# An attention and expert layer on one core: the idle TensorE products behind the loop are left out

## What is computed

```python
scores = jax.nn.sigmoid(x @ router_w.T)
G = jnp.einsum('ecd,edi->eci', Xp, W_gate)
U = jnp.einsum('ecd,edi->eci', Xp, W_up)
Y = jnp.einsum('eci,eid->ecd', jax.nn.silu(G) * U, W_down)
```

## The kernel before

| constant | products | place |
|---|---|---|
| WARM_HEADS | 3 | line 1316, ahead of the scores of head 2 |
| WARM_TILE | 2 | line 1339, ahead of the transposes of tile 1 |
| WARM_LAST | 3, twice | line 1341, behind the transposes of each tile |
| WARM_CHOICE | 3 | line 1368, behind `shared_hidden(0)` |
| WARM_ROWS | 4 | line 1376, behind the three products of the places |

## Time and profile before

### The profile page before, as it was taken

The page is one execution under the profiler, slowest core; times in us unless marked ns, Lnnn a source line. Parts: engine busy times, 40 slices in busy tenths (PEclk is TensorE's granted clock), DMA queues, the critical chain, the costliest instruction groups (busy, mean ns, idle before and its releaser), DMA issues.

```text
span 650.2 us, 15227 instructions
## 1 busy us (share of the span) xinstructions
PE 625.8 (96%) x6032; PEld 462.3 (71%) x6032; DVE 388.8 (60%) x554; ACT 363.6 (56%) x524; POOL 179.0 (28%) x146
## 2 busy tenths in 40 slices
PE   8999999999999999999999999999999999999976
PEld 5866666777777777777778777899556797564433
DVE  5979587766766766767767767556125885401001
ACT  4542765767677676676677667787123884311000
POOL 0260335354353353453443433300001231000000
PEclk9999999999999999999999999999999999999979
DMA  9943894224323323423422422500999006499995
GB/s 349 417 173 80 216 318 100 56 57 83 71 54 74 77 52 70 83 50 65 90 48 60 98 49 54 107 1 9 413 415 378 32 6 251 149 396 412 417 418 218
DMA packets 28072, 105.14 MB, mean 162 GB/s; under 512 B 4224, under 2 KB 8064, under 8 KB 22784
## 3 DMA queue, kind: packets, MB, share of 16 engines
q1 hardware_dynamic: 28032, 104.57, 50.3%
HBM read 77.29 MB, written 0.52 MB: 120 GB/s over the span
## 4 chain that ended last, share of the span: by engine, by line
PE 74%; DVE 8%; issue 5%; SPq 4%; ACT 4%; DMA 4%; POOL 1%; DVEq 0%; ACTq 0%
PE psO L1124 9%; PE psO L1135 9%; PE psO L1125 8%; PE psS L1111 8%; PE psS L1112 8%; PE psM L1083 5%; PE psO L1203 4%; PE psO L1067 3%; PE psS L1412 3%; DVE arena L779 2%; SPq L448 2%; PE psO L1069 2%; PE psO L1068 2%; DMA arena<-rope 2%; DMA arena<-w_exp 2%
## 5 line engine op out<-in xcount | busy, mean ns | idle before, releaser
L779 DVE TENSOR_REDUCE arena<-psM 128x2 f32<-128x1024 f32 x121 | 147.7, 1221 | 66.3 <-PE psM L1083 66.0
L588 ACT ACTIVATE arena<-psS 128x1024 bf16<-128x1024 f32 x128 | 131.4, 1026 | 87.5 <-PE psS L1112 85.4
L481 POOL TENSOR_TENSOR arena<-arena 128x1024 bf16<-128x1024 f32 x56 | 120.8, 2156 | 190.3 <-ACT arena L590 166.8
L1124 PE MATMUL psO<-arena 128*128 128x129 bf16 x1024 | 132.8, 220 | 0.3 <-DVE arena L797 0.3
L1125 PE MATMUL psO<-arena 128*128 128x128 bf16 x1024 | 132.4, 220 | 0.0
L590 ACT ACTIVATE arena<-psS 128x1024 f32<-128x1024 f32 x129 | 130.9, 1015 | 0.0
L1111 PE MATMUL psS<-arena 128*128 128x256 bf16 x512 | 120.5, 273 | 0.9 <-DVE arena L790 0.9
L1112 PE MATMUL psS<-arena 65*128 65x256 bf16 x512 | 120.8, 273 | 0.0
L1124 PEld LDWEIGHTS psO<-arena 128*128 128x128 bf16 x1024 | 99.1, 98 | 18.8 <-issue 11.2
L1125 PEld LDWEIGHTS psO<-arena 128*128 128x128 bf16 x1024 | 99.4, 97 | 6.8
L818 DVE TENSOR_TENSOR arena<-arena 128x1024 bf16<-128x1024 f32 (+1 forms) x73 | 88.0, 1207 | 15.4 <-ACT arena L590 15.3
(11 more groups left out here) (206 smaller groups left out, 747.3 us busy)
## 6 DMA issues: line engine op xcount, KB each, us to landing
arena<-w_exp SPq DMA_DIRECT2D x27, 1024.0 KB, 19.5
arena<-arena SPq DMA_DIRECT2D x96, 256.0 KB, 3.7
arena<-w_exp SPq DMA_DIRECT2D x31, 512.0 KB, 16.6
arena<-w_pair SPq DMA_DIRECT2D x8, 1088.0 KB, 19.1
arena<-w_exp SPq DMA_DIRECT2D x22, 256.0 KB, 6.4
arena<-w_o SPq DMA_DIRECT2D x1, 4096.0 KB, 21.6
arena<-ctx SPq DMA_DIRECT2D x4, 512.0 KB, 13.0
arena<-rope SPq DMA_DIRECT2D x4, 512.0 KB, 14.3
```

What stands on the lines that cost most here:

```text
L481: nc.gpsimd.tensor_tensor(p_lo[:, s % 2, :], p_f[:, s % 2, :], p_hi[:, s % 2, :], ALU.subtract).then_inc(s_plo[0], 1)
L588: nc.scalar.activation(p_hi[:, s % 2, :], psS[s % 2][:, :], ACT.Exp).then_inc(s_phi, 1)
L779: nc.vector.reduce_max(maxes[:, :, st, c], maxima_bank(q, m)[:, :].rearrange("p (j n) -> p j n", j=2), AX.X).then_inc(s_mfree, 1)
L1124: mm(psC[:, st, :], ph, vx[:, GROUP * g + i, 0:CW], start=g == 0 and i == 0 and st == 0, stop=False, skip_group_check=True)
```

## The change

The eighteen idle products behind the loop are left out: 3 + 2 + 2 x 3 + 3 + 4. The fourteen at the start stay. No other instruction, wait or transfer is changed.

```diff
--- before.py
+++ after.py
@@ -108,7 +108,7 @@
 DVE_BEFORE = order("rows0 q0 rows1 rope0 rows2 q1 k0 rows3 q2 rope1 m0 k1 rope2 rope3 k2 m1 m2 q3 k3 m3 m4 m5 q4 k4 m6 m7 m8 q5 "
                    "k5 m9 m10 k6 m11 m12 q6 m13 k7 m14 m15 q7")
 PAIR_BUFS = 6
-WARM_START, WARM_HEADS, WARM_TILE, WARM_LAST, WARM_CHOICE, WARM_ROWS = 14, 3, 2, 3, 3, 4
+WARM_START = 14
 
 
 def expert(k):
@@ -1312,8 +1312,6 @@
                     queries(h)
                 if 1 <= h <= TT:
                     values(h - 1)
-                if h == 3:
-                    warm(WARM_HEADS, psM[:, 0:512])
                 if 0 <= h - 1 < NH2:
                     scores2(h - 1)
                 if 0 <= h - 3 < NH2:
@@ -1335,10 +1333,7 @@
 
             pe.wait_ge(ld_route, 32)
             for st in range(TT):
-                if st:
-                    warm(WARM_TILE, psF[1])
                 xn_transposed(3, st)
-                warm(WARM_LAST, psF[1])
                 pe.wait_ge(ln_T, 2 * TT + st + 1)
                 for c in range(DC):
                     last = mm(psA[0][:, E * st:E * st + E], xnT[:, c, P * st:P * st + P], w_router[:, c, :], start=c == 0, stop=c == DC - 1)
@@ -1365,7 +1360,6 @@
                         mm(psO[n][:, D // 2 * st:D // 2 * (st + 1)], hs[:, i, P * st:P * st + P], sd[:, i, halves[n]],
                            start=i == 0 and st == 0, stop=False, skip_group_check=True)
             shared_hidden(0)
-            warm(WARM_CHOICE, psF[1])
             pe.wait_ge(sel_done, 1)
             pe.wait_ge(ld_const, 32)
             early, ones = const[:, C_EARLY:C_EARLY + P], const[:, C_ONES:C_ONES + P]
@@ -1373,7 +1367,6 @@
             mm(psA[1][:, 0:E], early, chosen[:, 0, :], start=True, stop=True)
             mm(psA[1][:, E:2 * E], ones, chosen[:, 0, :], start=True, stop=False)
             mm(psA[1][:, E:2 * E], early, chosen[:, 1, :], start=False, stop=True).then_inc(pos_mm, 1)
-            warm(WARM_ROWS, psF[1])
             pe.wait_ge(cleared, 2)
 
             def chosen_rows(part, c):
```

## The result

The changed kernel takes 654.69 us (653.22 to 655.73), beside 652.32 for the kernel before in the same series: ratio 1.0031, interval 1.0022 to 1.0040. It is slower by 2.4 us, inside the stated range of 651.2 to 654.9. They are not the quotients of the two medians, and differ from them by up to 0.1%.) The forecast had the wrong sign: no change, 0.2 us down. The profiled execution took 655.16 us.

The account below looks back on a forecast made before the run. The last 80 us were taken as one weight transfer, started when the first gate_up products free ring space. Six terms, five of 0 and one of 0.15 us, gave 651.9 against the profiled 652.05, 652.5 against the median; range 651.2 to 654.9.

Parts of the forecast that it names:

- the first release: First gate_up products free a quarter of four ring buffers at 563.5; only what moves this moves the end.
- HEADS: Three products at 505.66, ahead of head 2's score (L1267), which waits for GpSimd's L527: saved 0.
- CHOICE: Three products at 558.64, ahead of L1373, which waits for VectorE's choice of experts (L910): saved 0.
- TILE: Two products at 552.09, ahead of tile 1's transposes, which VectorE's L733 releases: saved 0, at most 0.05 us.
- both LAST: Three products at 550.33 and three at 553.36, ahead of the router's L1344, which waits for ScalarE's L546: saved 0.
- ROWS: Four products at 560.49 hold up L1385, which could start once the first one-hot (L952) is there: saved 0.15 us.
- D: All eighteen products lie open, the waits not being what the trace's releasers say: 3.9 us faster, 648.2; chance 0.06.
- I take it that the clock holds: Router stage, 549.9 to 555.1: the clock stays at 2.4 GHz though TensorE's busy share drops to 0.64; chance 0.56.
- B: Clock falls in the router stage, 553.4 to 555.4, for 6.8 us: +2.2 us, 654.25; +0.55 if half as long; chance 0.28.
- No DMA is moved: Whole kernel: no DMA moved and no wait added; expert 12's half and the stores stay, so no cost was counted.
- holes behind 566: Sign: holes in the DMA engines' full stretch behind 566 would refute the claim that only one release counts.
- E: Clock falls behind the gaps at 558.81 and 560.65; first gate_up takes twice its 0.99 us: +0.85, 652.9; chance 0.05.

Follow-up runs that it names:

- run 4: Changed kernel with half of shared_hidden(0) (its up part, 4 of 8 products) left out, output incomplete; 655.32 us against 652.39, ratio 1.0038.
- run 3: Kernel before with its eighteen idle products behind the loop kept in place, but 8 columns wide instead of 512; 654.48 us against 652.39, ratio 1.0034.
- run 1: Kernel before with only WARM_TILE and WARM_LAST kept of the eighteen; HEADS, CHOICE and ROWS left out; 653.11 us against 652.39, ratio 1.0016.
- run 2: Kernel before with only the eight idle products of the two router tiles (WARM_TILE, WARM_LAST) left out; 654.47 us against 652.39, ratio 1.0033.
- run 7: Changed kernel with the half of expert 12 issued by ScalarE's queue instead of the sync queue; 654.00 us against 652.57, ratio 1.0032.
- run 15: Kernel before, idle products included, with 220 satisfied waits more on TensorE in the first 60 us; 655.15 us, ratio 1.0038.
- control with 60: Kernel before with 60 satisfied waits more on TensorE in the first 60 us; 652.89 us, ratio 1.0006.
- run 13: Changed kernel with 60 satisfied waits more on TensorE in the first 60 us; 654.72 us against 652.35, ratio 1.0026.
- run 8: Kernel before with only the three idle products of WARM_CHOICE left out; 652.48 us against 652.57, ratio 1.0005.
- run 11: Kernel before with only the four idle products of WARM_ROWS left out; 652.82 us against 652.23, ratio 1.0006.
- run 5: Kernel before with one wait more in the sync queue, so the half of expert 12 is issued later; 653.64 us against 652.57, ratio 1.0010.
- run 10: The changed kernel measured again, unaltered; 654.14 us against 652.23, ratio 1.0027.
- run 16: The changed kernel measured a third time, unaltered; 654.67 us against 652.35, ratio 1.0028.
- run 9: Changed kernel with satisfied waits ahead of each tile's transposes, 18 instructions added instead of the 36 meant; 654.01 us against 652.23, ratio 1.0028.

## Why the prediction was wrong

**What bounds the kernel, and the way to the end: right.** Everything ahead of the first release comes through to the end (doubled `shared_hidden(0)`: 2.85 in, 2.87 out). That nothing can be saved in the tail was right too: the changed kernel's tail still waits for its weights.

**The six terms: right but for one size.** HEADS, CHOICE: 0, by their own runs (0.9998 and 1.0005). TILE and both LAST: 0; in the changed kernel L1007 and both L1339 start behind the releasers named, L733 and L546. ROWS: 0.06 and not 0.15. L1385 starts 0.45 us behind L952, when the first one-hot has been there for 0.15; what holds it for these 0.15 no run parts. D, all eighteen open, falls with them.

**The step that failed: "I take it that the clock holds".** It rested on comparing 5.2 us at a busy share of 0.64 with two stretches of other shapes at full clock, 0.74 and 0.54, and on no gap being over 1.0 us, when the only fall in the trace came in a standstill. Neither comparison carries over. The second of those rows is no safe case either: in the kernel without WARM_ROWS the clock fell at 643.5, at the end of such a stretch, of the same products (2.12 of 4.00 us busy from 639.6 on), though with longer gaps, up to 1.45 us. Instead of a clock that holds, the runs showed a fall to 1.2 GHz in eight of nine profiles without the eight products at full width: 6.8 us in three, 3.4 in four, 13.7 in that of run 4. The narrow products show that the work in the gaps decides, and runs 1 and 2 that the eight products of the router stage are the ones. For the two long falls B had the place (554.4; measured 554.0 to 554.5), the length (6.8 us) and the end of the dense group (562.2; 556.07 + 6.13 = 562.20). It gave +2.2 us; the two long falls cost 2.02 and 1.89. For a low level half as long it gave +0.55; the execution with 3.4 us shows 0.46, but otherwise than B had it: there L1339 is at full clock, L1351 ends 1.69 us late, and 0.99 of these are covered by the wait for L910. The chances, 0.56 for a clock that holds and 0.28 for B, were the wrong way round; no row of the trace had a stretch of this make at full clock.

The rule that the prediction cited against itself, in the Trainium skill, "TensorE: Matmul & The Clock Gate", section "A second HAM failure mode: psum-queue depth-cycling", holds here for the fall: the trace agrees, with a fall behind gaps of 0.5 to 0.7 us. A swing that repeats itself the runs do not show in this stage.

**The term that was missing: about 1 us.** "No DMA is moved" was true of the kernel's own transfers alone. The program's instructions come by DMA too, and one fetch moved from an idle moment onto the second issue. Two things move it there, each by itself: another count of instructions at full clock (run 7, and the 220 of run 15), and a low clock at the same count (run 3). The changed kernel has both. The prediction had named the sign ("holes behind 566"), and with it its claim that only the first release counts falls: the second issue stands on the same path. That a fetch moved onto the issues makes the second one long is shown by the kernel with 220 instructions, against its control with 60, and by all eighteen profiles (below). The cost is about 1 us by the means above, 0.96 against 0.31 in that pair of profiles. Why the issue waits for the fetch is open. So is where a fetch falls: with the clock low it came later than the count of instructions says (runs 3 and 13).

**E** was real, but does not show in the changed kernel: there the clock has just risen, from 561 on, when the gaps of the choice come (whether that is the reason was not tested). It shows when the router stage is repaired (run 1: first `gate_up` 1.85 us and not 1.06, medians +0.7 us). WARM_CHOICE and WARM_ROWS cover each other; either can go, not both, by runs 1, 8 and 11 (one profile each).

**The size.** The sum of B's +2.0 and the fetch's +1.0 would be 3.0, as in the profile of the result; the medians say 2.4, 1.9 and 2.3 in three series. The three profiles of the changed kernel show +3.06, +1.31 and +2.54: the low level lasts 3.4 us in one and 6.8 in two. No version tried beats the kernel before.

## What to carry to other kernels

An idle product that fills a wait saves nothing when it is taken out, and may be what holds the clock: ask what dense work on the critical path stands behind the gap, price it at half speed, and give that case a large chance when nothing dense is left in the stretch. One profile at full clock does not clear a stretch: here the router stage without its products kept the clock in one of nine. If such products must go, try them place by place, as here three of the five constants (WARM_HEADS, WARM_CHOICE, WARM_ROWS) can each be set to 0 alone at no loss that the runs can tell (up to 0.17% by the widest interval). And when instructions are added or removed, look where the program's own fetches land against the DMA issues that the end depends on.

## What the runs showed of the hardware

**A fetch beside an issue.** The packets of queue 8 and the second issues of the row (in run 5 the first quarter's, second behind the half), with their ends, in every profile in which the two overlap:

| kernel (run) | fetch, us | second issue, us | its end behind the fetch's |
|---|---|---|---|
| changed | 566.37 to 567.37 | 566.21 to 567.74 | 0.37 |
| changed, again (10) | 565.75 to 566.70 | 566.00 to 567.05 | 0.35 |
| changed, third (16) | 566.11 to 567.13 | 566.30 to 567.50 | 0.37 |
| router stage without (2) | 564.98 to 566.12 | 565.36 to 566.49 | 0.37 |
| narrow products (3) | 566.56 to 567.49 | 566.43 to 567.86 | 0.37 |
| half of expert 12 later (5) | 564.23 to 565.67 | 565.13 to 566.03 | 0.37 |
| half on ScalarE's queue (7) | 564.95 to 566.26 | 565.26 to 566.63 | 0.37 |
| without WARM_CHOICE (8) | 563.34 to 564.27 | 564.01 to 564.63 | 0.37 |
| changed, 18 more (9) | 564.27 to 565.55 | 564.53 to 565.92 | 0.37 |
| changed, 60 more (13) | 565.40 to 566.33 | 566.00 to 566.70 | 0.37 |
| before, 220 more (15) | 564.60 to 565.85 | 564.94 to 566.21 | 0.36 |

In the other seven profiles the fetch is over before the second issue starts, or comes long after it, and the issue takes 0.43 us; in the kernel before by 0.11 us only (563.87 and 563.98). So the second issue does not end until some 0.37 us after the packet, whatever its own start. The first issue of a row is not held: it takes 0.34 us beside a fetch too (563.60 before). Runs 9 and 13, whose times decide nothing, fit in with this.

The kernel before has the same thing once in its hardware loop. Three issues of one pass, of the 256 KB stores and loads of lines 363 to 365:

```profile
401.60 0.51 SPq L363 DMA_DIRECT2D arena<-arena  x1
402.15 1.22 SPq L364 DMA_DIRECT2D arena<-arena  x1
403.42 0.59 SPq L365 DMA_DIRECT2D arena<-arena  x1
```

L364 takes 0.50 to 0.60 us each of the eighteen times from 168 to 382 and 1.22 here, with a queue 8 packet that starts at 401.98 and ends at 402.99, 0.38 us ahead of the issue's end. Issues of 1.0 to 1.3 us are also seen at 66 to 69 and at 107 to 109, without a fetch there, so it is not the only cause.

**The length of a fall.** Of the falls between 554 and 565, five took 3.4 us of low level (runs 1, 2, 9, 10 and 13), three 6.8 (narrow products, changed kernel twice), and one 13.7; in one profile of a router stage without idle products there was none. One profile of such a kernel does not give its cost.

**Other falls come and go.** That of the earlier trace rows is missing in the changed kernel: its tail is at 1.00 from 624.0 to 630.5. What it costs there was not tested; the tail waits for weights anyway. The one at 643.5 to 650 of the kernel without WARM_ROWS, behind the last weights, went with an execution 2.2 us over that kernel's median.
